# Router folded into the dense feed-forward blocks, and Pool's bias additions moved behind the totals' store

## What is computed

```python
xf = input.reshape(N, Dq)                                 # N = 8192
eid = argmax(softmax(xf @ router_w + router_b))
onehot = one_hot(eid, E)
rank = cumsum(onehot, axis=0)[arange(N), eid] - 1
valid = rank < C
buf = zeros((E, C, Dq)).at[eid, pos].add(xf * vmask)      # pos = rank where valid
y = relu(buf @ w1 + b1) @ w2 + b2                         # per expert
yov = relu(xf @ ow1 + ob1) @ ow2 + ob2                    # for tokens without room
out = y[eid, pos] * vmask + yov * (1 - vmask)
```

## Time and profile before

| what | before |
|---|---|
| median of three runs (lowest to highest) | 2875.94 us (2864.01 to 2879.75) |
| the profiled execution, all of it | 2866.38 us |
| its span, first to last instruction | 2864.6 us |
| PE busy | 2667.4 us (93%) |
| DVE busy | 2035.7 us (71%) |
| ACT busy | 1827.5 us (64%) |
| POOL busy | 959.8 us (34%) |
| mean granted clock of TensorE | 0.961 |

### The profile page before, as it was taken

The page is one execution under the profiler, slowest core; times in us unless marked ns, Lnnn a source line. Parts: engine busy times, 40 slices in busy tenths (PEclk is TensorE's granted clock), DMA queues, the critical chain, the costliest instruction groups (busy, mean ns, idle before and its releaser), DMA issues. The chain is left out here.

```text
span 2864.6 us, 48122 instructions
## 1 busy us (share of the span) xinstructions
PE 2667.4 (93%) x16633; PEld 1604.8 (56%) x16633; DVE 2035.7 (71%) x3311; ACT 1827.5 (64%) x3442; POOL 959.8 (34%) x1021
## 2 busy tenths in 40 slices
PE   5899999875999999999999999999999589999997
PEld 3788999862333334334333333333333478899886
DVE  6654546746788898898888988978894655444674
ACT  5444556641787786887877868878777544444664
POOL 3354113533242332342423322422212325421353
PEclk9999999985999999999999999999999889999998
DMA  5211113424334244242342342423411522111342
GB/s 174 67 44 44 51 48 101 131 65 80 63 73 90 45 84 97 51 95 62 74 95 52 77 93 54 76 63 77 86 51 34 171 59 52 44 45 44 102 134 67
DMA packets 191746, 215.95 MB, mean 75 GB/s; under 512 B 56364, under 2 KB 152804, under 8 KB 191584
## 3 DMA queue, kind: packets, MB, share of 16 engines
q1 hardware_dynamic: 156176, 169.03, 25.0%
q0 software_dynamic: 35408, 44.84, 5.6%
HBM read 114.54 MB, written 48.57 MB: 57 GB/s over the span
## 5 line engine op out<-in xcount | busy, mean ns | idle before, releaser
L1534 DVE TENSOR_REDUCE at_mxc<-at_pb 128x2 f32<-128x1024 f32 x1024 | 1216.5, 1220 | 196.0 <-PE at_pb L1359 189.5
L1467 ACT ACTIVATE at_ex<-at_pd 128x512 f32<-128x512 f32 x2048 | 1075.7, 602 | 338.3 <-PE at_pd L1370 334.4
L1370 PE MATMUL at_pd<-at_qa,at_ka 50*128 50x512 f32 x2048 | 611.4, 472 | 5.3 <-ACT at_ex L1467 5.3
L1370 PEld LDWEIGHTS at_pd<-at_qa,at_ka 50*128 50x128 f32 x2048 | 270.8, 186 | 569.2 <-issue 411.6
L775 DVE TENSOR_TENSOR f_ml_hl<-f_ml_h,f_ml_hh 128x512 fp32r<-128x512 f32 (+1 forms) x384 | 263.6, 688 | 447.5 <-ACT f_ml_hh L851 385.5
L1379 PE MATMUL at_po<-at_ex,at_va 128*32 128x512 f32 x4096 | 552.9, 612 | 0.0
L848 ACT ACTIVATE f_ml_h<-f_ml_pL,b1T 128x512 f32<-128x512 f32 (+1 forms) x384 | 243.4, 634 | 450.9 <-PE f_ml_pL L902 382.6
L1359 PE MATMUL at_pb<-at_ka,at_qa 48*128 48x512 f32 x2048 | 416.6, 450 | 30.6 <-DVE at_mxc L1534 18.4
L917 PE MATMUL f_ml_pA<-f_wh,f_ml_hh 128*128 128x256 f32 (+1 forms) x1408 | 410.3, 291 | 2.2 <-DVE f_ml_hl L775 2.0
L919 PE MATMUL f_ml_pA<-f_wl,f_ml_hh 128*128 128x256 f32 (+1 forms) x1408 | 402.0, 286 | 0.4 <-issue 0.4
L920 PE MATMUL f_ml_pA<-f_wh,f_ml_hl 128*128 128x256 f32 (+1 forms) x1408 | 401.9, 285 | 0.0
(11 more groups left out here) (135 smaller groups left out, 2782.8 us busy)
## 6 DMA issues: line engine op xcount, KB each, us to landing
f_wraw<-in_L_ffn_w SPq DMA_DIRECT2D x128, 256.0 KB, 2.8
at_qa<-at_parts SPq DMA_DIRECT2D x384, 64.0 KB, 2.5
at_ka<-at_parts SPq DMA_DIRECT2D x384, 64.0 KB, 2.7
at_oscr<-at_os POOLq DMA_DIRECT2D x63, 256.0 KB, 2.4
f_ro_xr<-in_L_attn_x SPq DMA_DIRECT2D x16, 512.0 KB, 3.9
f_ml_xr<-in_L_attn_x SPq DMA_DIRECT2D x16, 512.0 KB, 4.2
x<-f_ml_yo SPq DMA_DIRECT2D x16, 512.0 KB, 3.9
at_xr<-x SPq DMA_DIRECT2D x16, 512.0 KB, 4.9
```

The costliest lines, as they stand in the source:

```text
L1370: eng.matmul(pd[n % RING][:, :], ka[g][rows, p, kt * P:(kt + 1) * P], qa[g][rows, qh, p, :], start=True, stop=True).then_inc(s_full.sem, 1)
L1467: eng.activation(ex[t % 2][:, j, :], pd[n % RING][:, :], ACT.Exp).then_inc(s_free[n % RING].sem, 1)
L1534: eng.tensor_reduce(mxc[:, t // NT, kh, t % NT::NT], pb[kh][:, :].rearrange("p (e k) -> p e k", e=2), AX.X, ALU.max, negate=True).then_inc ...
```

## The change

`router`, `Slots` and the Fori loops go. The new `mlps` is one block of programs, written out over STEPS = all (n, s), and g = 8 n + s numbers the steps. Tables say what else happens in which step. A block's rows are turned up to three blocks ahead, which takes four buffers (`DEEP`) for the row parts, and `pT` is one bank now. The other bank, `pR`, holds products, logits and counts of the block that is being routed. The router's products are taken from the high and the low row parts that the dense blocks need anyway.

```diff
+class Route:
+    EXPERTS, SLOTS = 11, 6
...
+    def done(self, u, ops):
+        return self.s_v.at((self.EXPERTS + self.SLOTS) * u + ops)
...
+    def products_step(self, eng, u, high, low):
+        if u > 0:
+            eng.wait_ge(self.s_v.sem, self.done(u - 1, 13))
+        for f in range(DT):
+            for part in (high, low):
+                for j in range(4):
+                    mm = eng.matmul(self.products[RW * j:RW * (j + 1), :], self.k.rw[:, f, :],
+                                    part[:, f, j * P:(j + 1) * P].bitcast(F32),
...
+    def count_step(self, eng, u):
+        eng.wait_ge(self.s_v.sem, self.done(u, 12))
...
+        eng.matmul(self.counts, self.k.tri[:, :], flat(self.onehot), start=True, stop=False)
+        eng.matmul(self.counts, self.k.ones[:, :], flat(self.so_far[u % 2]),
+                   start=False, stop=True).then_inc(self.s_counts.sem, 1)
...
+        turned_at = {1: 3, 5: step(3, 4), 10: step(7, 4)}
+        turned_at.update({u: step(u - 1, 0) for u in (2, 3, 4)})
+        turned_at.update({u: step(u - 2, 0) for u in (6, 7, 8, 9)})
+        turned_at.update({u: step(u - 3, 0) for u in range(11, NB)})
+        turned_at.update({u: step(u - 1, 0) for u in range(NB, NB + E)})
+        TURN = {g + 2 * f: (u, f) for u, g in turned_at.items() for f in range(DT)}
+        STATS = {g - 5: u for u, g in turned_at.items()}
+        APPLY = {g - 3: u for u, g in turned_at.items()}
+        routed_at = {0: 0, **{u: g + 4 for u, g in turned_at.items() if u < NB}}
+        PRODUCTS = {g: u for u, g in routed_at.items()}
+        LOGITS = {g + 1: u for u, g in routed_at.items()}
+        EXPERTS = {g + 2: u for u, g in routed_at.items()}
+        COUNTS = {g + 3: u for u, g in routed_at.items()}
+        SLOTS = {g + 4: u for u, g in routed_at.items()}
+        BIAS = {2: 0, **{step(n, 1) if n else 5: n + 1 for n in BLOCKS if n + 1 < NB + E}}
...
         @block.gpsimd
...
+            for n, s in STEPS:
+                g = step(n, s)
+                if s == 0 and n > NB:
+                    scatter(n - NB - 1)
+                if g in SLOTS:
+                    puts(SLOTS[g])
+                if g in BIAS:
+                    with_bias(BIAS[g])
+                if g in STATS:
+                    norm.pow_step(eng, STATS[g], len(rows_of[kind_of(STATS[g])]))
+                if s == 4 and n >= NB - 3 and n + 3 < NB + E:
+                    gather(n + 3 - NB)
+                if s == 6 and split_at(n):
+                    weights_low(split_at(n))
```

```diff
                     if past and t % NT == 5:
                         totals_out(*past)
+                    if g == 3 and t % NT == 5:
+                        eng.wait_ge(s_xl.sem, s_xl.at(16 * (8 + b + 1)))
...
                     if past and t % NT == 6:
                         totals_in(*past)
...
-                    if g == 3 and t in (4, 12):
-                        eng.wait_ge(s_xl.sem, s_xl.at(16 * (8 + b + 1)))
```

More of the change, by code:

```diff
@@ L523, in mlps @@
     LAG = 3
+    DEEP = 4
     LOW = "VVVVVVVG"
@@ L596, in split_at @@
-        def split_at(i, n, b, kind):
-            if kind == "expert":
-                return None if isinstance(n, int) and n == NB + E - 1 else (2 * i + b + 1, b)
-            return (0, 1) if isinstance(n, int) and n == NB - 2 else None
+        kind_of = lambda n: "dense" if n < NB else "expert"
+        BLOCKS = range(NB + E)
+        STEPS = [(n, s) for n in BLOCKS for s in range(HT)]
+        step = lambda n, s: HT * n + s
+        turned_at = {1: 3, 5: step(3, 4), 10: step(7, 4)}
+        turned_at.update({u: step(u - 1, 0) for u in (2, 3, 4)})
@@ L662, in _ @@
+            store(NB - 1)
+            for m in range(3, E + 1):
                 for q in range(PIECES):
-                    load_piece(e, q, of_expert(w1, e), of_expert(w2, e))
+                    load_piece(m, q)
         @block.gpsimd
@@ L830, in _ @@
-            stream(eng, prologue, block_)
+            stats(0)
+            weights(0, 0)
+            apply(0)
+            weights(0, 1)
+            for f in range(DT):
+                rows_low(0, f)
+            for q in (2, 3):
+                weights(0, q)
+            for h in range(LAG):
+                hidden_low(0, h)
+                weights(0, PIECES // 2 + h)
+            stats(1)
+            for n, s in STEPS:
+                g = step(n, s)
+                if g in TURN:
+                    rows_low(*TURN[g])
+                if s + LAG < HT:
+                    hidden_low(n, s + LAG)
+                elif n + 1 < NB + E:
+                    hidden_low(n + 1, s + LAG - HT)
+                if split_at(n):
+                    for q in pieces_at(s):
+                        weights(split_at(n), q)
+                if g == 1:
+                    half_biases()
+                if g in SLOTS:
+                    route.slots_step(eng, SLOTS[g], put)
+                if g in STATS:
+                    stats(STATS[g])
+                if g in EXPERTS:
+                    route.experts_step(eng, EXPERTS[g])
+                if g in APPLY:
+                    apply(APPLY[g])
+                if s == HT - 1:
+                    results(n)
```

722 lines of the change are left out of this document (269 added, 453 removed).

## The result

The changed kernel takes 2834.8 us (median of 4 runs, 2831.4 to 2846.3) where the kernel before took 2873.4 (median of 4, with one more run than was shown ahead): a ratio of 0.9878, 95% interval 0.9847 to 0.9909. The fall of the medians is 38.6 us, where the prediction's sum has 16.5. The profiled executions differ by 32.6 us (spans 2864.6 and 2832.0), and this is what the traces can account for. All times and ratios leave out one slow execution, of experiment 5, which took 3232.8 us at a mean clock of 0.727.

A forecast was written before the change was run, and what follows sets the result against it. Dense blocks were taken as bound by TensorE, the router's pass by loading and vector work. From 2875.9 us, -120 - 8 + 47 + 49.5 + 20 + 43 - 48 = -16.5 gave 2859.4 us, range 2797 to 2913.

The forecast's parts named there:

- The start: Up to block 0's first result: the router's pass goes, -60 us a feed-forward, -120 in all, 5 either way each.
- TensorE's added work: Dense blocks: product, logit-turning and count matmuls add 1.55 us a block, +47 us in all.
- The wait for the counts: Dense blocks: TensorE waits 1.65 us at the count matmuls for DVE's small operations, +49.5 us in all.
- The wait for the room: Blocks turned four steps apart: products wait 2.45 us for the shared bank, four times a pass, +20 us.
- The clock: TensorE drops to 1.2 GHz behind every product wait and half the count waits, 1.86 us each, +43 us.
- the gain of 8: Dense blocks 1 to 8: four Pool puts a block in place of eight win back 3.9 us a pass, -8.
- Rival 1: Dense blocks: counts nearly in time, wait 0.8 us, clock stays; -53 on top, 2806 us; chance 0.17.
- rival 2: Dense blocks: every count wait costs the clock; +28, 2887 us; chance 0.18.
- The expert blocks: Pool's bias additions moved to step 1 save about 4.0 us a block, for six of eight blocks: -48 us.
- Rival 3: Expert blocks keep their period, Pool's additions in step 1 making DVE late; +48, 2907 us; chance 0.27.
- Attention: Pool's two additions go behind the totals' store, DVE meets them a step later: 0, 3 us either way.
- The sum: Whole kernel: all terms together give -16.5 us, so 2859.4 us from 2875.9.

The follow-up runs named there:

- experiment 5: Changed kernel with Pool's old order in the expert blocks: biases behind the power, gather behind the weight piece; 2873.2 us, ratio 1.0043.
- experiment 8: Changed kernel with count matmuls and slot operations one step later and routings at least six steps apart; 2760.7 us, ratio 0.9623.
- Experiments 4 to 6: Changed kernel, Pool's expert-block order partly or wholly reversed: biases behind the power, 2852.7 us; also gather behind weight piece, 2873.2; gather move alone, 2839.3.
- experiment 7: Changed kernel with the turns of blocks 5, 6, 10 and 11 one or two steps later, counts unmoved; 2822.2 us, ratio 0.9838.
- experiment 2: Kernel before with only the attention part of the change, Pool's additions behind the totals' store; 2854.7 us, ratio 0.9953.
- experiment 10: The changed kernel itself, unedited, timed again on the chip of the version with all mends; 2846.8 us, ratio 0.9892.

## Why the prediction was right, step by step

**The start** (-60 a pass, 5 either way): -54.8 and -54.3, just outside the 5. The first L759 stands at 21.23, not 20.0. Up to the first transposes the sum was right (16.11, and 16.08 by its terms), since rows that came 0.4 us earlier than reckoned made up for Pool's first power, 1.42 us where I had 1.05. What failed is the price of the one bank: the way from the transposes to L759 is 5.12 us, 2.46 more than the 2.66 before and not 1.3, because the second half goes through the whole chain of transposes, copy and low part behind the first. The first block then took 41.6 us where I took 37.5, since its waits are longer than the later ones, 2.41 at the counts, 1.70 at a later first-layer matmul, and the first of them cost the clock.

**TensorE's added work** (1.55 us a block): 1.79 by experiment 8, +54 and not +47. Block 14, without a routing, took 22.56 us and not 23.4, since no transposes fall in it either. The 16 products take 1.01 us from the first to the matmul behind them where I had 0.80 from the weight loads; the rest is where they join the stream.

**The wait for the counts** (1.65 us): 1.46 in nearly every block (2.41, 2.01 and 1.68 in the first three), 45.2 us without block 0's two, for 49.5. The sum of small operations was right; the working from one step's clock times was good to 0.2 us. Moving it a step showed that it was a matter of place only.

**The wait for the room** (2.45 us, 8 times): 2.36, 8 times, 18.9 us.

**The clock** (+43): this term was taken too high by its half of the count waits. TensorE's clock in the 3 us behind waits of 2.41, 2.01, 1.68, 1.46 and 2.36 us:

```profile
43.50:46.50 3.00, 3.00 (x14) 3.00 (x15) 2.91 (x12) 0.00 (x0) 0.00 (x0) 0.50 0.00 0
73.60:76.60 3.00, 3.00 (x16) 3.00 (x17) 1.07 (x2) 0.00 (x0) 0.00 (x0) 0.55 1.04 328
93.10:96.10 3.00, 3.00 (x20) 3.00 (x21) 2.33 (x4) 0.60 (x1) 0.00 (x0) 0.71 0.70 117
121.60:124.60 3.00, 3.00 (x24) 2.87 (x25) 2.92 (x12) 0.60 (x1) 0.43 (x1) 1.00 0.00 0
155.70:158.70 3.00, 3.00 (x38) 2.62 (x34) 0.54 (x4) 0.28 (x1) 1.30 (x2) 0.52 0.74 259
```

The 1.46 that nearly all blocks have cost no clock. From block 0's result to block 15's the granted clock falls short of 1.00 by 10.2 us a pass, summed over time, so the term was 20 and not 43. Of the +137.4 between block 0 and block 15, 53.7 are work, 45.2 and 18.9 the two waits; 19.6 are left for the clock, for the 0.30 us beside each count wait (30 x 0.30 = 9) and for the gain of 8 that I had from the puts. With 20.4 for the clock that adds up to within 2 us (20.4 + 9 - 8 = 21.4), so the gain is likely; it was not tested by itself. I had gone by the 1.70 of attention, next to which I put 1.65; 1.46 lay on the side of the 0.98. Rival 1 had that half right (no clock at the counts) and the wait wrong (0.8 us); rival 2 is out.

**The expert blocks** (period 16.5 to 17, -48): 17.1 on average, and -39.9. The term was too large in its saving per block, 4.0 where some 3.5 came (20.6 to 17.1). TensorE's own work in a block is 16.96 us at a clock of 1.00 (mean of the four blocks from 500.50 to 569.60), not 16.5; so behind the wait of 2.2 the low clock cost 20.63 - 2.2 - 16.96 = 1.5 us and not 1.86. The account of the cause was half right. I laid all of DVE's lateness to the bias additions, the first normalisation's 1.46 us in the earlier trace rows too, which Pool's weight piece stretched. Experiments 4 to 6 show that either of the two moves taken back costs 11.5 or 8.0 us of the two passes, both together 34.9 of the 39.9. The diff moved the gather, and the prediction did not price it: a step moved on Pool counted for me as DMA issue, when it was what kept an addition away from the normalisation. The last 5.0 us are not explained. Rival 3 (the additions in step 1 make DVE late there) did not happen: a low part in step 1 takes up to 2.3 us beside them, one of the weights up to 3.0, and DVE's free time takes it up.

The rule of the Trainium skill that I weighed ("GPSIMD Engine Reference", section "1. Specifications") agrees with these rows for the low parts and the subtraction, which have two SBUF inputs and which Pool's additions stretch. The cast and the normalisation are stretched as well, with one such input each; by the rule they would have to run in a two-port mode, which no run here shows. I took from it only that the contention moves with the additions; what counts is which operation of DVE it moves to.

**Attention** (0, 3 either way): -19.9 in the trace, and the step that failed. I wrote that DVE "meets the same additions a step later" and priced a meeting the same wherever it is. Beside the chain of short operations that ends a step it costs up to 2.6 us, TensorE waits (8.9 us less of it now) and drops its clock in four places; beside the long reductions over PSUM it costs nothing. The row for it was at hand: behind the wait of 1.70 us in the earlier trace rows I never asked what DVE had been late with.

**The sum.** Start +11, dense blocks -14, expert blocks +8, attention -20, the rest -1: together -16 under -16.5, and that is -32.6. The terms missed by more than the sum did, and that is luck: in the feed-forward the misses of 11, 14 and 8 us cancel to 5. Nothing cancels the 20 of attention, which make the fall twice the forecast; the range of 116 us took it in.

## What to carry to other kernels

When an operation of Pool on SBUF is moved, list what VectorE runs at the old and at the new place. In this case casts and subtractions were held or stretched beside it, and reductions were not; the DMA issues between Pool's operations are part of that placing. Where TensorE waits for a short chain on VectorE, first try the consumer one step later: here that gave 2.6% beyond the change together with wider spacing of the turns, for a few numbers in tables, and the respacing has to leave room for both ends of the chain, as experiment 7 shows. And before a span is compared with a span, see that the clock was the same in the stages that were not edited.

## What the runs showed of the hardware that was not expected

A cast of 16 elements a partition from SBUF, 0.175 us alone, took up to 2.83 us beside Pool's two-input additions, to 0.04 us behind their end; copies on Pool, with one input and 0.62 us long each, held it to their end in the same way, for 0.37 us at most. Reductions of 1024 elements out of PSUM kept their 1.22 us, and it is not shortness or PSUM that decides: the reduction of 32 elements out of SBUF just ahead of the cast kept its 0.19 us beside the additions in 11 places of the kernel before.

A TensorE wait costs more than its idle time even where the clock stays: 1.76 us a block for 1.46 idle. The expert blocks of the changed kernel agree: without a wait TensorE is busy for 16.70 and 16.80 us, with one of 0.3 to 0.54 for 16.97 to 17.06.

The last 60 us of attention run at a different granted clock from one execution to another, of one kernel too. It was 1.00 in the traces of the kernel before, of the changed kernel and of experiment 2, and fell to 0.50 in the other nine, some 30 to 50 us before the last transposes. The 135 us up to the last transposes, in the changed kernel as first profiled and in experiment 10:

```profile
2056.00:2191.00 135.00, 129.05 (x773) 45.62 (x774) 94.45 (x104) 106.75 (x207) 29.76 (x40) 1.00 0.14 40
```
```profile
2068.00:2203.00 135.00, 130.88 (x681) 44.05 (x680) 80.61 (x93) 94.27 (x182) 26.63 (x35) 0.85 0.12 34
```

The 0.85 is a mean: the first 75 us of that window have 1.00, the last 60 have 0.66. From the second wait to the last transposes attention takes 1514.4 us in the first of these traces and 1530.3 in the second, so this is 16 us, as much as what was looked for in several experiments. In its last 40 to 50 us TensorE waits some 0.45 us for ScalarE's exponentials in every 2.6 us, where the clock stays at 1.00 as well as just before a fall, so these waits alone do not tell why one execution falls and another does not. It stays open.
